# Attention weighings cut into two query halves, with a new turning of the sums, a new order on TensorE and the expert weights loaded in pieces

## The reference

```python
h = layernorm(x) * (1 + ca) + sa
# 16 heads of 8; each head keeps only its 819 best keys (40% of 2048), chosen by a router
scores = sigmoid(sigmoid(relu(h @ r_w1.T + r_b1) @ r_w2.T + r_b2))      # per token and head
keep   = top_k(scores of a head over all tokens, 819)
attn   = where(keep, q @ k.T / sqrt(8), -1e30)
x = x + ga * (softmax(attn) @ v)
h = layernorm(x) * (1 + cb) + sb
# 8 experts, top 1: relu(h @ fc)^2 @ proj, of the expert with the largest probability
x = x + gb * moe(h)
```

## Time and profile before

| what | value |
|---|---|
| median of 3 runs | 523.1 us |
| lowest, highest | 515.16, 523.27 us |
| profiled execution: its own time | 519.57 us |
| its span, first to last instruction | 517.7 us |
| its mean granted TensorE clock | 0.878 |
| TensorE busy | 438.4 us (85%) |
| VectorE busy | 393.6 us (76%) |
| ScalarE busy | 310.5 us (60%) |
| GpSimd busy | 218.8 us (42%) |

### The profile page before, as it was taken

One profiled execution on the slowest core, in us unless ns is written; L12 is line 12 of the kernel. 1 busy time (PEld: TensorE's weight loads), 2 busy tenths in 40 slices (PEclk: granted clock), 3 DMA queues, 4 the chain that ended last, 5 costly groups with the idle time before them and its releaser, 6 DMA issues.

```text
span 517.7 us, 9420 instructions
## 1 busy us (share of the span) xinstructions
PE 438.4 (85%) x3253; PEld 213.1 (41%) x3253; DVE 393.6 (76%) x1063; ACT 310.5 (60%) x457; POOL 218.8 (42%) x301
## 2 busy tenths in 40 slices
PE   3677557779999999999999999999999967089873
PEld 3342442223343343434433343334334327089872
DVE  8788948868898898689768967889889944836551
ACT  2435200357777778577657856777877863057662
POOL 2200274425346358348535824445100400077775
PEclk9878555599999999899879978999999995579998
DMA  8032600540100100010010010010000004022210
GB/s 246 3 122 68 158 7 4 184 150 4 35 4 5 36 5 5 4 36 3 5 35 4 4 35 5 5 31 8 3 2 2 22 1 143 0 74 57 66 30 21
DMA packets 20208, 21.11 MB, mean 41 GB/s; under 512 B 5741, under 2 KB 15793, under 8 KB 20161
## 3 DMA queue, kind: packets, MB, share of 16 engines
q1 hardware_dynamic: 14704, 16.12, 10.4%
q0 software_dynamic: 5168, 4.00, 3.9%
q10 hardware_dynamic: 288, 0.39, 0.2%
HBM read 14.41 MB, written 7.27 MB: 42 GB/s over the span
## 4 chain that ended last, share of the span: by engine, by line
PE 65%; DVE 15%; DMA 7%; issue 6%; POOL 3%; ACT 2%; SPq 0%; POOLq 0%; DVEq 0%; ACTq 0%
PE OP L1513 17%; PE ST L1497 12%; PE ST L1473 6%; DVE tile_max L1079 6%; PE SC L1451 6%; PE SC L1449 4%; PE ST L1645 3%; PE SC L1634 2%; DMA KV<-rows_dram,owner 2%; PE OP L1521 2%; DMA QS<-MT 2%; DVE PR L949 2%; DMA C<-in_const 1%; PE OP L1600 1%; PE ST L1403 1%
## 5 line engine op out<-in xcount | busy, mean ns | idle before, releaser
L1079 DVE TENSOR_REDUCE tile_max<-SC 128x1 f32<-128x410 f32 (+1 forms) x512 | 270.9, 576 | 55.5 <-PE SC L1449 51.2
L801 ACT ACTIVATE PR<-ST 128x1024 f32<-128x1024 f32 (+1 forms) x224 | 207.7, 961 | 52.0 <-PE ST L1497 51.3
L565 POOL DMA_INDIRECT G<-kv_dram,idx x104 | 107.4, 1033 | 169.6 <-ACT PR L801 93.6
L1497 PE MATMUL ST<-QS,KT 51*128 51x512 bf16 (+1 forms) x416 | 108.7, 397 | 4.5 <-DMA QS<-MT 4.2
L1513 PE MATMUL OP<-PR,VS 128*32 128x512 f32 x768 | 107.5, 633 | 0.4 <-ACT PR L801 0.4
L1449 PE MATMUL SC<-KT,QS 48*128 48x410 bf16 x256 | 79.3, 365 | 1.8 <-ACT KT L767 1.0
L1497 PEld LDWEIGHTS ST<-QS,KT 51*128 51x128 bf16 (+1 forms) x416 | 29.1, 96 | 54.2 <-issue 36.6
L1451 PE MATMUL SC<-KT,QS 48*128 48x409 bf16 x128 | 46.5, 364 | 3.6 <-DVE tile_max L1079 0.3
L696 POOL DMA_INDIRECT KV<-rows_dram,owner x23 | 24.7, 1073 | 50.5 <-DVE owner L1285 43.8
L1453 PE MATMUL SC<-KT,QS 48*128 48x358 bf16 x128 | 43.3, 338 | 0.7 <-DVE tile_max L1079 0.7
L1473 PE MATMUL ST<-C,OS 128*128 128x32 f32 x248 | 38.8, 281 | 0.2
(11 more groups left out here) (257 smaller groups left out, 533.2 us busy)
## 6 DMA issues: line engine op xcount, KB each, us to landing
kv_dram<-KV SPq DMA_DIRECT2D x4, 512.0 KB, 2.9
WE<-in_w_fc SPq DMA_DIRECT2D x1, 2048.0 KB, 9.9
WE<-in_w_proj SPq DMA_DIRECT2D x1, 2048.0 KB, 14.9
G<-kv_dram,idx POOLq DMA_INDIRECT x104, 2.4
q_parts_dram<-QP SPq DMA_DIRECT2D x3, 512.0 KB, 3.7
QS<-q_parts_dram SPq DMA_DIRECT2D x16, 96.0 KB
X<-in_x SPq DMA_DIRECT2D x4, 256.0 KB, 6.7
QS<-q_parts_dram SPq DMA_DIRECT2D x16, 64.0 KB
```

What stands on the lines that cost most here:

```text
L565: pool.indirect_dma_start(G[:, i % 2, slot_of(s), :], None, kv_dram, bass.IndirectOffsetOnAxis(ap=idx[:, i, s:s + 1].bitcast(U32), axis=0) ...
L801: nc.scalar.activation(PR[:, k, 0:cols], ST[:, (KSTEPS * n + k) % 2, 0:cols], ACT.Exp, scale=float(D) ** -0.5).then_inc(exp_done, 1)
L1079: v.tensor_reduce(tile_max[:, n % 2, at_col:at_col + 1], bank(RING_AT["unit", u])[:, 0:410 - f], AX.X, ALU.max).then_inc(s_reduced, 1)
L1497: last = mm(ST[:, at_step % 2, 512 * e:512 * e + 512], KT[rows, i % 2, P * tile:P * tile + P], QS[rows, i % 2, CHUNK * c:CHUNK * (c + 1)], ...
```

## The change

- A weighing takes a half of 256 queries for each call; a chunk has six calls and the shared one, and pv_done rises by WEIGHS = 7 for each chunk instead of 4. All waits on it are recounted.
- The four partial sums are added first (sum_o): "sum_groups" (128x32) is the stationary side, a 128-column piece of OS the moving side, four products into four groups of 32 partitions. ScalarE copies the 128x128 result to OSUM (copy_sum), and TensorE turns it with one transposition (turn_o). copy_ot stays.
- The order on TensorE is written out anew. The scores of step 0 and one tile of step 1 stand before the end of the turn before, as does the wait for the mask rows. 30 units are made before the loop (LEAD) instead of 28.
- The expert weights come in 16 transfers, each one expert's half (256 KB), one behind the mask rows of each of the first 16 chunks.

```diff
-LEAD = 28
+WEIGHS = 7
+LEAD = 30
...
-            for n, w_part in enumerate((w_fc, w_proj)):
-                sp.dma_start(WE[:, :, HD * n:HD * (n + 1)], w_part.rearrange("n p c -> p n c"))\
-                    .then_inc(we_in, 16)
+            def load_expert(piece):
+                at, half = piece // 2, piece % 2
+                sp.dma_start(WE[:, at, HD * half:HD * (half + 1)], (w_fc, w_proj)[half][at]).then_inc(we_in, 16)
             for n in range(NCH):
...
                 if n + 1 < NCH:
                     m_rows(n + 1)
+                if n < 2 * NE:
+                    load_expert(n)
...
+            def copy_sum(n):
+                act.wait_ge(osum_done, n + 1)
+                if n >= 1:
+                    act.wait_ge(otr_done, n)
+                nc.scalar.activation(OSUM[:, :], turned_o(n), ACT.Copy).then_inc(osum_copied, 1)
...
-                weights(n, 2, 3)
-                weights(n, 3, 2)
+                weights(n, 2, 5)
+                if n >= 1:
+                    copy_sum(n - 1)
+                weights(n, 3, 3)
...
-            def turn_o(n, tiles):
+            def sum_o(n):
                 pe.wait_ge(o_copied, n + 1)
-                for t in tiles:
-                    last = mm(turned_o(n)[:, 32 * t:32 * t + 32], OS[:, P * t:P * t + P], cc("sum_groups"),
+                for t in range(4):
+                    last = mm(turned_o(n)[32 * t:32 * t + 32, :], cc("sum_groups"), OS[:, P * t:P * t + P],
                               start=True, stop=True)
-                if tiles[-1] == 3:
-                    last.then_inc(otr_done, 1)
+                last.then_inc(osum_done, 1)
+
+            def turn_o(n):
+                pe.wait_ge(osum_copied, n + 1)
+                nc.tensor.transpose(turned_o(n), OSUM[:, :], ident).then_inc(otr_done, 1)
...
-            def weigh(n, steps_, first=False):
+            def weigh(n, steps_, half, first=False):
...
+                q0 = CHUNK // 2 * half
                 for g in range(4):
                     k, e = steps_[g // 2], g % 2
                     tile = 2 * (k - (k > 3)) + e
-                    last = mm(OP[32 * g:32 * g + 32, :], VS[:, i % 2, tile, :], PR[:, k, 512 * e:512 * e + 512],
+                    last = mm(OP[32 * g:32 * g + 32, q0:q0 + CHUNK // 2], VS[:, i % 2, tile, :],
+                              PR[:, k, 512 * e + q0:512 * e + q0 + CHUNK // 2],
                               start=first, stop=False, skip_group_check=True)
...
+            scores(0, 0, 1, first=True)
+            scores(0, 0, 0, last=True)
+            scores(0, 1, 1, first=True)
             for n in range(NCH):
...
+                scores(n, 1, 0, last=True)
                 unit()
+                if n >= 1:
+                    weigh(n - 1, (5, 6), 1)
+                unit()
+                unit()
+                if n >= 1:
+                    weigh(n - 1, (5, 6), 0)
+                scores(n, 2, 1, first=True)
+                unit()
+                scores(n, 2, 0, last=True)
+                unit()
+                scores(n, 3, 0, first=True, last=True)
+                if n >= 1:
+                    sum_o(n - 1)
+                unit()
+                unit()
+                weigh(n, (0, 1), 0, first=True)
+                if n >= 1:
+                    turn_o(n - 1)
...
+                if n + 1 < NCH:
+                    turn_m(n + 1)
+                scores(n, 4, 1, first=True)
+                unit()
+                scores(n, 4, 0, last=True)
+                unit()
+                weigh(n, (0, 1), 1)
+                scores(n, 5, 1, first=True)
+                unit()
+                scores(n, 5, 0, last=True)
+                unit()
...
+                weigh_shared(n)
+                scores(n, 6, 1, first=True)
+                unit()
+                scores(n, 6, 0, last=True)
+                unit()
+                weigh(n, (2, 4), 1)
+                if n + 1 < NCH:
+                    scores(n + 1, 0, 1, first=True)
+                unit()
+                if n + 1 < NCH:
+                    scores(n + 1, 0, 0, last=True)
+                unit()
+                weigh(n, (2, 4), 0)
+                if n + 1 < NCH:
+                    scores(n + 1, 1, 1, first=True)
+                unit()
```

More of the change, by code:

```diff
@@ L56 @@
 TURN_AT = {(2, 0): 1}
-TURN_AT.update({(NQ * (i - 1) + 1, 14): i for i in range(2, NP)})
+TURN_AT.update({(NQ * (i - 1) + 1, 11): i for i in range(2, NP)})
 AHEAD = 5
@@ L400, in build @@
         kt_ready = sem("kt_ready")
+        osum_done = sem("osum_done")
+        osum_copied = sem("osum_copied")
         otr_done = sem("otr_done")
@@ L829, in _ @@
             copy_o(NCH - 1)
+            copy_sum(NCH - 1)
             copy_ot(NCH - 1)
@@ L1468, in turn_m, with scores @@
                 nc.tensor.transpose(turned_m(n), NMB[:, 1::2], identb[:, :]).then_inc(mtr_done, 1)
-            def turn_o(n, tiles):
+            def sum_o(n):
                 pe.wait_ge(o_copied, n + 1)
-                for t in tiles:
-                    last = mm(turned_o(n)[:, 32 * t:32 * t + 32], OS[:, P * t:P * t + P], cc("sum_groups"),
+                for t in range(4):
+                    last = mm(turned_o(n)[32 * t:32 * t + 32, :], cc("sum_groups"), OS[:, P * t:P * t + P],
                               start=True, stop=True)
-                if tiles[-1] == 3:
-                    last.then_inc(otr_done, 1)
-            def scores(n, k, e, first):
+                last.then_inc(osum_done, 1)
+            def turn_o(n):
+                pe.wait_ge(osum_copied, n + 1)
+                nc.tensor.transpose(turned_o(n), OSUM[:, :], ident).then_inc(otr_done, 1)
+            def scores(n, k, e, first=False, last=False):
                 i, c = n // NQ, n % NQ
@@ L1496, in scores @@
                 tile = 6 if k == 3 else k - (k > 3)
[L1497 to L1500, removed]
-            def weigh(n, steps_, first=False):
+                product = mm(ST[:, at_step % 2, 512 * e:512 * e + 512], KT[rows, i % 2, P * tile:P * tile + P],
+                             QS[rows, i % 2, CHUNK * c:CHUNK * (c + 1)], start=True, stop=True)
+                if last:
+                    product.then_inc(st_filled, 1)
+            def weigh(n, steps_, half, first=False):
                 i = n // NQ
@@ L1553, in unit @@
                         score_unit(units.pop(0))
[L1555 to L1568, removed]
-                        if n - 1 in LIST_BESIDE:
-                            row_to_partition(LIST_BESIDE[n - 1])
-                        if n + 1 < NCH:
-                            turn_m(n + 1)
-                        continue
-                    scores(n, k, e, True)
-                    unit()
-                    scores(n, k, 1 - e, False)
-                    unit()
-                    if k == 1:
-                        if n >= 1:
-                            weigh(n - 1, (5, 6))
-                        unit()
-                    if k == 4:
-                        weigh(n, (0, 1), first=True)
-                        unit()
-                    if k == 5:
-                        weigh_shared(n)
-                        if n % NQ == 1 and NQ < n < NQ * (NP - 1):
-                            turn_k(n // NQ + 1)
-                    if k == 6 and n == 1:
-                        turn_k(1)
@@ new lines, in _ @@
+                unit()
[6 more added lines that the diff above has]
+                unit()
+                if n % NQ == 1 and NQ < n < NQ * (NP - 1):
+                    turn_k(n // NQ + 1)
+                weigh_shared(n)
+                scores(n, 6, 1, first=True)
+                unit()
+                scores(n, 6, 0, last=True)
@@ L1595, in _ @@
-            turn_o(NCH - 1, (0, 1, 2, 3))
+            weigh(NCH - 1, (5, 6), 1)
+            weigh(NCH - 1, (5, 6), 0)
+            sum_o(NCH - 1)
+            turn_o(NCH - 1)
             def route(g):
```

29 lines of the change are left out of this document (18 added, 11 removed).

## The result

The changed kernel takes **484.9 us** (median of 4 runs, 483.48 to 486.31) against 523.2 (515.16 to 523.76) for the kernel before, run on the same chip: a ratio of 0.936, 95% interval 0.925 to 0.946. The profiled execution is 484.94 us with a span of 483.1, 34.6 us shorter than before's 517.7. The forecast was 490, the range 480 to 508. Executions of one kernel show a faster and a slower state; ratios compare runs of the faster one alone, medians and ranges are of all runs.

A forecast was written before the change was run, and what follows sets the result against it. TensorE and VectorE were taken to hold each other up, neither full. Chunks falling from 9.48 to 8.52 us gain 26.9 over 28, the start 4: 519.57 comes to 488.7, rounded to 490; range 480 to 508.

The forecast's parts named there:

- step 1: Weighings cut from three of 512 columns to six of 256 at 0.573 us each: +0.44 us a chunk.
- step 2: Turning of the sums by four products, a copy and one transposition instead of eight thin products: -0.56 us a chunk.
- step 3: New TensorE order: lone units become pairs, -0.54 us a chunk, and shorter absences remove bank waits, -0.40.
- Rival C: Half a weighing costs nearly a whole one: no gain from 0.75 us, at 0.85 a time of 533; chance 0.04.
- step 4: Next chunk's first scores may wait for mask rows, up to 0.2 us a chunk, taken as 0.1: chunk 8.52.
- sum of 8.42: TensorE's pieces in one chunk after the change, in us, at or just above VectorE's 8.1 to 8.4.
- step 5: Expert weights in sixteen pieces free the second chunk's mask rows at the start: 4 us gained.
- Rival E: Pieces do not free the mask rows, or the start gains nothing otherwise: 494, inside the forecast; no separate chance.
- rival B: Clock holds near the index products where it fell, giving back up to 10 us: 480 to 487; chance 0.14.
- D: Many short drains lower the clock through the whole loop: at 0.85, chunk 10.0 and time 530; chance 0.05.
- the rest: Counts behind GpSimd's copies of V and later banks for key turnings cost nothing while gathers lie ahead.
- Rival A: New waits for sums, mask rows and banks, 0.2 us each, make a chunk 9.1 and the time 505; chance 0.14.

The follow-up runs named there:

- the last experiment: Changed kernel with the keys' gathers asked for earlier, plus the odd half's mask rows sent first with their own semaphore: 479.83 us, ratio 0.927.
- both joined versions: Changed kernel with the shared weighing directly behind a half weighing, 490.48 us; the same with gathers asked for earlier and odd half's mask rows first, 488.57 us.
- its repeat: The changed kernel run once more, unchanged: 486.06 us, ratio 0.934 to the kernel before.
- two loads: Changed kernel with the expert weights again in two transfers of 2 MB ahead of the second chunk's mask rows: 494.59 us, ratio 0.956.
- earlier gathers: Changed kernel with the gathers of the next pair's keys paced closer together, the last five score steps earlier: 481.16 us, ratio 0.922.
- the repeat of the earlier gathers: The changed kernel with the keys' gathers asked for earlier, run once more without further change: 481.54 us, ratio 0.928.

## Why the prediction was right

**The half weighing** (step 1, 0.573): 0.57. The straight line between 128 and 512 columns holds at 256, so about 0.147 us of each such visit does not grow with its columns. The Trainium skill's "TensorE: Matmul & The Clock Gate", section Single matmul latency, would make it 0.593 as an estimate, since its figure is for one bf16 product on the whole array; the trace sides with the line. The rule of the Trainium skill's "TensorEngine Tiling (Array Packing)", Key Properties, that a change of tiling mode drains TensorE agrees with there being a fixed part; no run shows that the drain is what it is.

**The turning** (step 2, -0.56): products 0.36 as said, transposition 0.25 for 0.20, copy 0.28 for 0.25; so -0.51 of work.

**Pairs and banks** (step 3, -0.54 and -0.40): the pairs take 0.33 and 0.28 (170.56 to 170.89, and behind a half weighing), and neither engine waits for long in a plain chunk. VectorE's starving went as forecast, but the prediction wrote the parts as terms that add up, and alone they do not:

| what is changed | plain chunk | against 9.48 |
|---|---|---|
| order alone | 9.51 | +0.03 |
| cut alone | 9.69 | +0.21 |
| new turning alone | 9.17 | -0.31 |
| order and new turning | 9.45 | -0.03 |
| order and cut | 8.93 | -0.55 |
| all three | 8.49 | -0.99 |

(Cut and new turning in the old order were not run.) By the prediction's pieces TensorE has 1.1 us less to do with order and new turning than before, and the chunk is the same: VectorE starves 0.92 us in it as before (0.90), and TensorE stands still for 1.02 (exponentials 0.35, a bank 0.33, the sums' copy 0.34). That whole weighings make any work taken off TensorE worthless is not shown: in the old order the new turning gave 0.31. In the new order it gives 0.06 with whole weighings, where its copy is waited for, and 0.44 with half ones, which stand between the copy and its use. So the cut seems to pay twice, by shorter absences (0.58 with the thin turning) and by cover for the copy. Whole weighings at other places of the new order were not tried. Rival C, half weighings too dear, is refuted by the 0.57.

**Mask rows late** (step 4, 0.1): the wait is there, 0.08 behind one half weighing a chunk, worth 0.03 to 0.05 by the last experiment. The chunk shown is 0.12 over the sum of 8.42: this 0.08, the transposition's 0.05 and the pairs' 0.07 (0.61 for 0.54), less the shared tile's 0.04 (0.32 for 0.36) and smaller differences.

**Pieces and start** (step 5, 4): 3.8 from the first mask's turning on, and no wait of chunk 1 for mask rows. The other 1.7 of the 5.5 is no effect of the change. From profile to profile this stretch varies: in the ten with pieces it takes 15.6 to 18.0 us, longest where the half clock of the start lasts longest (to 107.8 us), against 19.6 before. A piece lands in 2.7 to 2.9 us, under the 6.7 that bounded it. In the new order the pieces are worth more than that, 8.1 counted the same way: TensorE asks for the rows 12.5 us after the first mask's turning (before 13.9), they come 1.2 later than before, and half clock follows. Rival E is refuted.

**The clock** (rivals B and D): B's mechanism came on top of the forecast, 4.9 us; none of the falls of before is there in the profiled execution. But its reason, the thin products ahead of the index work, is not the whole: of three chunks with index products the clock fell in three before and with the cut alone, in two with the thin turning in the new order and also in two with the new turning in the old order, in one each with whole weighings, with the order alone and in both joined versions, and in none of the changed kernel, its repeat, two loads, earlier gathers and odd rows first; in the repeat of the earlier gathers it fell once (203.4 us). Nearly all falls stand in versions whose engines wait longer for each other (VectorE idles 0.33 to 1.2 us in a plain chunk of theirs, 0.12 to 0.13 in the others), but what brings one on was not settled, and the repeat shows that it is not sure to stay away. This counts one profiled execution of each; the other runs of the changed kernel's repeat have mean clocks of 0.877 to 0.894 and up to 489.62 us, so falls in some of them are not excluded. D did not come: the granted clock is 1.00 from 101.8 to 388.5 us, through all the short visits. By the Trainium skill's "TensorE: Matmul & The Clock Gate", section A second HAM failure mode, short idling between groups of products lets the clock swing; this trace does not show that.

**What was wrong** is the sentence on "the rest", that the key turnings cost "nothing while the gathers lie ahead by most of a chunk". Chunks a microsecond shorter use that lead up, since a gather does not get faster with them: in chunks 5 and 9 TensorE waited about 1 us for the keys and nothing was gained, and in chunk 10 and the three behind index products it waited 0.33 to 0.53 for mask rows or a maximum, which earlier gathers take off too. In all that was 3.3 us in the loop, by the repeat beside the earlier gathers. Rival A's new waits came mostly in this place; of the three that it named, the mask rows cost something. Against the prediction's 488.7 the profiled execution is 3.8 us shorter: 4.9 by the clock and 1.7 ahead of the first mask's turning, less 2.0 in the two chunks with key turnings, 0.6 at the end and 0.2 at the start. So its mechanism bears out, and that 484.9 lies at the forecast's lower end (484 to 498), where rival B's 480 to 487 lies as well, is owed to the clock and to chance.

## What to carry to other kernels

Where two engines feed each other through a few buffers, look at the longest stretch in which one does not serve the other before taking work off either: here 1.1 us less of work in the new order did nothing with whole weighings, and the cut, which adds work, was worth 0.58 to 0.96 there. In the old order, with one unit or none between the halves, it cost 0.21, so a cut needs something to put between. After a speed-up, go through every producer that was paced by step numbers, such as the gathers' list, since their lead shrinks with the step. Price an edit's parts together where they share a wait, and test at least one of them alone.

## What was not expected of the hardware

```profile
q0 software_dynamic: 32, 0.01, 3.0%
q8 instruction: 1, 0.02, 2.3%
```

The same stands in the repeat (packet to 178.15, last part at 178.13) and with two loads (187.53, 187.52). With earlier gathers the fetch was over before the last of them; before, it met the last gather but one (packet 185.10 to 186.08, last part at 186.34). It is no single case. A gather has 16 packets of 512 bytes. In the fourteen traces between 60 and 420 us, 81 gathers that stand apart from others had the fifteenth begun while such a fetch still had 0.15 us or more to run: the sixteenth began within 0.03 us of the fetch's end in 72 of them, earlier in 5, later in 4. In the 1126 others it follows the fifteenth by 0.03 us in the median, and by over 0.25 in 28. No run moved the fetches, so the cause is argued from these times.

**Half the clock after a wait for mask rows.** With two loads TensorE stood 5.33 us and the granted clock was at half from inside the wait to 6.5 us past its end (106.5 to 116.7 us); the two together cost 8.1 us. Before, the wait of 2.69 us at the same place brought no such fall. But the length of the wait does not tell these apart. The other two kernels with transfers of 2 MB, the cut alone and the new turning alone, waited less there,

```profile
108.26 0.39 PE L1497 MATMUL ST<-QS,KT 51*128 51x512 bf16 x1 [2.15 <-DMA QS<-MT]
```

```profile
109.73 0.61 PE L1512 MATMUL ST<-QS,KT 51*128 51x512 bf16 x1 [2.35 <-DMA QS<-MT]
```

and had half clock from 108.6 to 125.7 and from 109.4 to 126.5 us. So it came in three of the four kernels with two large transfers and in none of the ten with pieces, which have no such wait; what keeps it away in the fourth is open.
